# Every order table of a five-engine GNN kernel is redrawn: head, first, steady, last and end

## The chip, the cores and the metric

One core of a Trainium2 chip runs the program. The metric is the device time of one execution in microseconds. A median of three executions stands for a kernel; one more execution was taken with the profiler. TensorE appears as PE (weight loads as PEld), VectorE as DVE, ScalarE as ACT, GpSimd as POOL, and SyncE, which issues the DMAs, as SP.

## The reference, cut to what matters

Two graph layers over 128 graphs (NB) of 128 nodes (N) and 64 features (F), 192 hidden columns (H) in the first.

```python
mask = (adj > 0.0)                                  # layer 0
h = relu((x @ W1a)[:, :, None] + (x[:, :, None] - x[:, None]) @ W1b + b1)   # each pair j, k
x = layernorm(x + einsum('bjkh,bjk->bjh', h, mask) @ W2 + deg * b2)
m = relu(relu(x @ W1 + b1) @ W2 + b2)               # layer 1
msg = relu(adj @ m)
r, z = sigmoid(i_r + h_r), sigmoid(i_z + h_z)       # i from msg, h from x
x = layernorm(x + (1 - z) * tanh(i_n + r * h_n) + z * x)
```

## The kernel before

**Tiling.** Graphs are taken four at a time: q = 0..31 (NQ = 32) is a quad. Layer 0 does not visit all pairs of nodes. For each quad a table of neighbours is made, and nine rounds of matmuls gather one neighbour each into PSUM; VectorE then does accumulator = accumulator + max(PSUM, 0). A quad has two halves, A (accumulator AC, `round_a`) and B (accumulator BB, `round_b`). Of each half ScalarE does round 1 (a plain relu, L1602 and L1618), VectorE rounds 2 to 9 (L1203 and L1223). Rounds 2 to 6 are 1152 columns wide, rounds 7 and 8 768, round 9 480.

**Turns.** Turn t (0 to 32) runs half B of quad t-1 and half A of quad t side by side: b1, a1, b2, a2, ... b9, a9. While VectorE accumulates one half's round from its PSUM banks, TensorE makes the other half's next round. Around these go, for other quads and groups of eight graphs (g, u):

- `prep(t+1)` (letter p): `x_split`, `ov`, `rank_t`, `rank_ov`, `words` (VectorE, tile WM, L1172), `x_turn`, `v` and `v_low` twice, `v_out` (SP copies VN to VA and VB), `surplus`. The DMA of `words` fills CW, from which `dgen(t, m)`, m = 0..3 (digits 0 to 3; VectorE, tile DM, L1182), makes the one-hot tables of turn t. `dgen(t, 0)` is needed by b1 and a1 of turn t, `dgen(t, 1)` by b2 and a2, and so on. On POOL the step `dgen` is a wait: POOL does not go on before that DM is made.
- `seeds(t)` (letter s): the first PSUM contents of half A of quad t, made after b9 of the turn before; ScalarE takes them off (L1626) before a1 may write.
- `parts_of_u` (b), `tail` (t: `s_ov`, `out0_a`, `out0_b`, `out0_c` of quad t-2), `ranks` (r: `mask`, two `rank_n`, `split_x`, `count`, `off`), `load` (l).
- layer 1 of a group of eight graphs, some 30 steps (`layer1_steps`): squares1, power1, scale1, xg, m1, m2, msg, the gates, tanh, gd, h, yt, y, squares2, power2, scale2, store. It starts in an odd turn (n) and is carried over the next turns (d, e).

**Order.** Each engine is in order. One list of steps made by `main_order` is followed by all five, so a letter's place in a table sets where the step stands in each engine's queue. `HEAD` is all before the first round; `FIRST` is turn 0; `ORDER[0]` the even turns and `ORDER[1]` the odd ones up to turn 30; `LAST` turns 31 and 32; `END` all after. A turn's table has 19 strings: one before b1, then one after each round of b and of a in turn.

**Banks.** PSUM banks 0 to 5 hold the rounds. All other matmul steps share banks 6 and 7: a step may write when the step that had the bank before has been taken off by its reader. The class `Banks` hands them out in the list's order, so a moved step also changes who waits for whom.

Of the kernel before, what the change touches and what calls it, by code (L numbers as in the profile page):

```python
# [53 lines left out]


ORDER = (
    ("e2p3bs", "", "rpbbd", "", "t", "p", "e", "rrp", "bt", "ptt", "pee", "edbpe", "pp", "e", "pd", "b", "d", "0", "1er"),
    ("bsb2", "", "3d", "pp", "btb", "p", "dd", "p", "tlpt", "etd", "bnbdrd", "dp", "depdn", "p", "p", "dp", "dpnr", "0", "1"),
)

FIRST = ("", "srr2hbp", "prb3", "b", "p", "", "hp", "", "bpb", "pp", "r", "pb", "r", "p", "0", "p", "p", "", "h1r")

LAST = (
    ("bbt", "b2s3dtb", "tt", "nd", "nbd", "ddn", "dbd", "nd", "", "d", "n", "d", "n", "", "ne", "de", "d01", "", "d"),
    ("bbdtb", "e", "etee", "e2dtftdnddnd", "dn", "fdded3ndde", "nf", "", "", "f", "bbn", "", "n", "", "", "df", "ene", "", "ddeb"),
)

HEAD = ("t", "WwL", "AASrXK", "EGrrr", "rr", "Mpp", "tpA", "wrtp", "ppr", "p", "ppfp0", "1pt")

END = ("d", "d", "tdlttttnndlnnn", "l", "ldnl", "l", "n", "ln", "ndnln", "llnnldt", "nl", "llnd", "lnlnnln", "l")  # L70

MAIN = (
# [119 lines left out]
def build(nc, adj, adjt, xt, xn, xq, w1, w2, rows, wg, cst, out):  # L192
    ctx = ExitStack()
    with ctx:
# [233 lines left out]
        def main_order(do):  # L428
# [82 lines left out]
            def checks():  # L511
                for k in range(5):
                    do("flag", k)
                    yield
# [31 lines left out]
            def halves(stage, n):  # L546
                for i in range(n):
# [5 lines left out]
                            "f": ("fold",), "0": ("dgen", 0, 0), "1": ("dgen", 0, 1)}  # L553
            for c in "".join(HEAD):
                if c in first_steps:
# [8 lines left out]
            for t in range(NQ + 1):  # L564
# [10 lines left out]
                if t == NQ:  # L575
                    link["n"] = layer1_steps(do, bank, NG - 1)
                    link["f"] = checks()
                order = FIRST if t == 0 else ORDER[t % 2] if t < NQ - 1 else LAST[t - NQ + 1]

# [40 lines left out]

            for c in "".join(END):
                if c in link:
# [1422 lines left out]
```

## Time and profile before

| what | us |
| --- | --- |
| median of 3 executions (812.18 to 813.53) | 813.08 |
| the profiled execution | 811.95 |
| its span, first to last instruction | 807.4 |
| start of turn 0's first accumulation on VectorE | 33.1 |
| one even and one odd turn in the steady part (turns 16 and 17) | 46.27 |
| last accumulation of half B, then the rest of the program | 785.2, 22.2 |

VectorE is the busiest engine; TensorE and ScalarE are not far behind. From turn 6 to turn 29 the trace repeats to a few hundredths of a microsecond from pair to pair, but for turns 21 and 23, so one pair stands for the steady part. In a timeline a row is: start in us, us from start to end, engine, line, operation, tiles out<-in, shapes, count, and in brackets the idle time before it with what ended it.

### The profile page before, as it was taken

What the parts mean: (1) busy time and instruction counts of PE and PEld (TensorE: products, weight loads), DVE (VectorE), ACT (ScalarE), POOL (GpSimd) and SP (SyncE); (2) the same over time, 40 slices, a digit from 0 to 9 for tenths busy, and PEclk for the clock granted to TensorE, in tenths of its full rate; (3) what the DMA queues carried; (4) which work ended last, traced back from release to release, by engine and by line L of the source; (5) the groups of instructions that cost most, each with busy time, mean ns of one, the idle gap of its engine ahead of it and who ended that gap; (6) DMA issues with size and microseconds to landing.
All of it is one profiled execution on the core that took longest, in us unless ns stands there. A gap on an engine that the chain in (4) does not pass through costs nothing.

```text
span 807.4 us, 37453 instructions
## 1 busy us (share of the span) xinstructions
PE 686.1 (85%) x15984; PEld 575.6 (71%) x15984; DVE 741.4 (92%) x817; ACT 674.4 (84%) x1931; POOL 610.7 (76%) x655
## 2 busy tenths in 40 slices
PE   1678779889898989989898898889889898989775
PEld 0557667778787877778777777777777787778653
DVE  4798989999999999999999999999999999998884
ACT  3857577889989989998989989898898999898664
POOL 4354555897979788897988889798888979776872
PEclk9999999999999999999999999999999999999998
DMA  4341322323233242323233242313324231222000
GB/s 168 84 129 42 105 69 55 106 64 106 49 93 81 56 120 69 100 68 100 57 76 103 64 119 55 115 35 100 89 56 115 65 109 45 59 68 55 16 15 27
DMA packets 33317, 62.67 MB, mean 78 GB/s; under 512 B 5504, under 2 KB 14464, under 8 KB 33152
## 3 DMA queue, kind: packets, MB, share of 16 engines
q1 hardware_dynamic: 33152, 60.29, 27.3%
q8 instruction: 126, 2.06, 1.1%
q14 instruction: 39, 0.32, 0.1%
HBM read 22.52 MB, written 4.19 MB: 33 GB/s over the span
## 4 chain that ended last, share of the span: by engine, by line
PE 44%; ACT 27%; issue 14%; DVE 11%; POOL 2%; DMA 1%; POOLq 0%; SPq 0%; DVEq 0%; ACTq 0%
PE PS L653 34%; PE PS L910 5%; PE PS L975 4%; DVE BB L1223 4%; DVE AC L1203 3%; ACT AC L1602 3%; ACT BB L1618 3%; ACT VN L1571 2%; ACT NNB L1586 2%; ACT SD L1626 2%; ACT NNB L1583 2%; ACT YO L1490 2%; ACT X L1407 1%; ACT XT L1558 1%; ACT Q L1505 1%
## 5 line engine op out<-in xcount | busy, mean ns | idle before, releaser
L1223 DVE SCALAR_TENSOR_TENSOR BB<-PS,BB 128x1152 f32<-128x1152 f32 (+4 forms) x256 | 293.0, 1145 | 29.2 <-PE PS L653 27.2
L1203 DVE SCALAR_TENSOR_TENSOR AC<-PS,AC 128x1152 f32<-128x1152 f32 (+4 forms) x256 | 292.2, 1141 | 1.9 <-PE PS L910 1.9
L653 PE MATMUL PS<-DM,VA 128*64 128x192 fp8e5 (+1 forms) x2048 | 127.5, 243 | 36.1 <-ACT SD L1626 18.5
L653 PEld LDWEIGHTS PS<-DM,VA 128*64 128x64 f16 x2048 | 82.8, 109 | 70.0 <-DVE AC L1203 28.0
L653 PE MATMUL PS<-DM,VB 128*64 128x192 fp8e5 (+1 forms) x2048 | 124.9, 241 | 0.3
L1182 DVE TENSOR_SCALAR DM<-CW 128x1536 uint16<-128x1536 uint16 (+1 forms) x132 | 112.3, 881 | 1.0 <-DMA CW<-WM 1.0
L1862 POOL TENSOR_TENSOR SD<-SD,BB 128x512 f32<-128x512 f32 (+1 forms) x62 | 77.9, 1275 | 36.1 <-DVE DM L1182 36.1
L910 PE MATMUL PS<-DM,VB 128*64 128x192 fp8e5 (+1 forms) x1024 | 85.7, 242 | 22.4 <-DVE BB L1223 17.2
L653 PEld LDWEIGHTS PS<-DM,VB 128*64 128x64 f16 x2048 | 91.1, 111 | 1.0 <-DVE BB L1223 0.5
L910 PE MATMUL PS<-DM,VA 128*64 128x192 fp8e5 (+1 forms) x1024 | 84.4, 240 | 0.4 <-DVE AC L1203 0.2
L910 PEld LDWEIGHTS PS<-DM,VB 128*64 128x64 f16 x1024 | 50.0, 110 | 40.5 <-issue 21.0
L1854 POOL TENSOR_TENSOR SD<-SD,AC 128x512 f32<-128x512 f32 x64 | 64.2, 1004 | 0.0
L1832 POOL TENSOR_TENSOR XE<-XQ,XT 128x512 f16<-128x512 f32 x32 | 37.6, 1176 | 30.8 <-ACT XT L1558 15.9
L1847 POOL TENSOR_TENSOR SD<-SD,NNB 128x512 f32<-128x512 f32 x64 | 58.1, 921 | 0.0
L1800 POOL TENSOR_SCALAR MT<-AT 128x1024 bf16<-128x1024 f32 x15 | 41.8, 2785 | 19.5 <-PE PS L653 18.7
L910 PEld LDWEIGHTS PS<-DM,VA 128*64 128x64 f16 x1024 | 50.8, 110 | 1.5 <-DVE AC L1203 1.2
L653 PE MATMUL PS<-w2s,SD 128*64 128x64 f32 (+1 forms) x768 | 48.2, 250 | 0.0
L1537 ACT ACTIVATE AM<-PS 64x512 int16<-64x512 f32 x64 | 37.6, 588 | 11.6 <-PE PS L653 11.0
L975 PE MATMUL PS<-w2s,AC 128*64 128x64 f32 x512 | 36.4, 225 | 4.0 <-ACT MS L1437 3.5
L975 PEld LDWEIGHTS PS<-w2s,AC 128*64 128x64 f32 x512 | 32.3, 138 | 9.8 <-ACT MS L1437 6.3
L1571 ACT ACTIVATE VN<-PS 128x384 f16<-128x384 f32 x64 | 31.6, 493 | 7.5 <-PE PS L653 6.2
L653 PEld LDWEIGHTS PS<-w2s,SD 128*64 128x64 f32 x768 | 37.7, 138 | 0.0
(243 smaller groups left out, 2203.7 us busy)
## 6 DMA issues: line engine op xcount, KB each, us to landing
CW<-WM SPq DMA_DIRECT2D x128, 160.0 KB, 2.8
XQ<-in_xq SPq DMA_DIRECT2D x32, 256.0 KB, 2.6
AT<-in_adjt SPq DMA_DIRECT2D x15, 512.0 KB, 4.0
VA<-VN SPq DMA_DIRECT2D x64, 96.0 KB, 2.2
VB<-VN SPq DMA_DIRECT2D x64, 96.0 KB, 2.2
XN<-in_xn SPq DMA_DIRECT2D x16, 256.0 KB, 4.1
out<-YO SPq DMA_DIRECT2D x15, 256.0 KB, 3.1
WG<-in_wg SPq DMA_DIRECT2D x1, 515.5 KB, 5.9
```

The costliest lines, as they stand in the source:

```text
L653: last = e.matmul(o[k], lhs[:, k], rhs, **flags)
L910: last = e.matmul(PS[h:h + 64, b + 2, 256 * (i // 2) + cols.start:256 * (i // 2) + cols.stop], lhs[:, i, k:k + 64], d[:, i, :], start=Fals ...
L975: last = e.matmul(PS[64 * h:64 * h + 64, b, 64 * i:64 * i + 64], lhs, w2s[:, w, :], start=(w == 0), stop=(w > 0))
L1182: e.tensor_scalar(DM[m][:, halves], CW[t % 3][:, halves, first], 6 - 2 * m, 0xC0C0, ALU.logical_shift_left, ALU.bitwise_and).then_inc(s["d ...
L1203: e.scalar_tensor_tensor(t, tiles(PS[:, b + p:b + 3, :])[:, :, cols], 0.0, t, ALU.max, ALU.add).then_inc(s["sx"], 1)
L1223: e.scalar_tensor_tensor(t, tiles(PS[:, r, :])[:, :, cols], 0.0, t, ALU.max, ALU.add).then_inc(s["sy"], 1)
L1537: e.activation(graphs(am[k])[:, :, 64 - 64 * h:192 - 64 * h], src[k], ACT.Copy, scale=2.0, bias=-258.0)
L1571: e.activation(VN[q % 2][:, 0, k:4:2, 0:H], PS[:, b, :].rearrange("p (a n) -> p a n", a=2)[:, :, 0:H], ACT.Copy).then_inc(s["vh"], 1)
L1800: e.tensor_scalar(MT[g % 3][:], AT[g % NA][:], 0.0, None, ALU.is_gt).then_inc(s["mask"], 1)
L1847: e.tensor_tensor(u, u, NNB[:, 4 * k:4 + 2 * k, :], ALU.mult).then_inc(s["im"], 1)
L1854: e.tensor_tensor(u, u, AC[q % 3][:, h, nat], ALU.add).then_inc(s["aa"], 1)
L1862: e.tensor_tensor(u, u, BB[q % 2][:, h, 0:128], ALU.add).then_inc(s["ad"], 1)
```

## The change

The five order tables are replaced. No step is added, removed or altered, and no function is touched; what changes is the place of each step in the five queues and, by that, which of banks 6 and 7 it gets.

```diff
 ORDER = (
-    ("e2p3bs", "", "rpbbd", "", "t", "p", "e", "rrp", "bt", "ptt", "pee", "edbpe", "pp", "e", "pd", "b", "d", "0", "1er"),
-    ("bsb2", "", "3d", "pp", "btb", "p", "dd", "p", "tlpt", "etd", "bnbdrd", "dp", "depdn", "p", "p", "dp", "dpnr", "0", "1"),
+    ("2se", "3b", "rppe", "", "bdb", "t", "p", "p", "ebe", "per", "pt", "rteptre", "p", "dp", "b", "d", "pbe", "", "01r"),
+    ("sl", "bb", "23t", "bd", "", "bppp", "ddbe", "p", "pttb", "tpr", "dnnd", "dd", "pnd", "p", "dn", "p", "", "dp", "dp01e"),
 )
-FIRST = ("", "srr2hbp", "prb3", "b", "p", "", "hp", "", "bpb", "pp", "r", "pb", "r", "p", "0", "p", "p", "", "h1r")
+FIRST = ("sph2", "3", "pbb", "", "", "bbp", "", "pb", "", "r", "pb", "rrr", "pp", "r", "ph", "p", "p", "0p", "1hr")
 LAST = (
-    ("bbt", "b2s3dtb", "tt", "nd", "nbd", "ddn", "dbd", "nd", "", "d", "n", "d", "n", "", "ne", "de", "d01", "", "d"),
-    ("bbdtb", "e", "etee", "e2dtftdnddnd", "dn", "fdded3ndde", "nf", "", "", "f", "bbn", "", "n", "", "", "df", "ene", "", "ddeb"),
+    ("bbts", "bdtb2", "", "ttnb", "ddn3", "e", "bdddn", "dddn", "", "d", "", "dn", "d", "", "end", "", "01n", "", ""),
+    ("fbbtbfde", "efet2ebf", "3", "ettn", "dnddddd", "ned", "e", "", "", "fdn", "den", "nbd", "", "", "ndd", "n", "", "bddee", ""),
 )
-HEAD = ("t", "WwL", "AASrXK", "EGrrr", "rr", "Mpp", "tpA", "wrtp", "ppr", "p", "ppfp0", "1pt")
-END = ("d", "d", "tdlttttnndlnnn", "l", "ldnl", "l", "n", "ln", "ndnln", "llnnldt", "nl", "llnd", "lnlnnln", "l")
+HEAD = ("L", "Xrr", "SrAAEWrrK", "rrG", "tArw", "ppw", "tp", "ptpt", "p", "f", "M", "p", "ppp0p1")
+END = ("ld", "ltllllt", "ltnt", "ntndlnl", "nd", "nllnltn", "nnld", "ldlnll", "dnn", "nd", "lnn", "nn", "nd")
```

Read out for one even turn, 16, the lists give (a slot is what stands behind the round named):

- before: a1 rank_n, ov; a2 s_ov; b3 rank_t; a3 split_h; b4 rank_ov; a4 out0_a; b5 words, out0_b, out0_c; a5 x_turn, yt twice; b6 y, xg, v, squares2; a6 v_low, v; b7 squares2, power2; a7 v_low, m1; a8 m2; b9 dgen(17, 0); a9 dgen(17, 1), off, v_out, surplus, seeds(17).
- after: a1 rank_n, x_split, ov, split_h; a2 xg; b3 s_ov; a3 rank_t; b4 rank_ov; a4 yt twice; b5 words, y, rank_n; a5 x_turn, out0_a; b6 split_x, out0_b, squares2, v, out0_c, count, squares2, power2; a6 v_low; b7 m1, v; b8 m2; a8 v_low; a9 dgen(17, 0), dgen(17, 1), off, v_out, surplus, seeds(17).

At the end of an odd turn, 17: before, surplus, scale1 and rank_n stand after a8, dgen(18, 0) after b9, and after a9 dgen(18, 1), h, dgen(18, 2), x_split(19), dgen(18, 3), seeds(18); msg stands before b2 of the odd turn. After: tanh and v_low stand after b9; after a9 gd, v_out, surplus, dgen(18, 0) to (18, 2), seeds(18), h, then b1, dgen(18, 3); msg stands behind b2, and s_ov before it. In the head, the mask's loads now stand first and the weights' later, and `wide_w(0)` behind `off` on VectorE.

## Rows read from the trace of the kernel before

**Rows 1.** The page's first part: busy us (share of the span) x instructions

```profile
PE 686.1 (85%) x15984; PEld 575.6 (71%) x15984; DVE 741.4 (92%) x817; ACT 674.4 (84%) x1931; POOL 610.7 (76%) x655
```

**Rows 2.** Windows of turns 16 and 17: stretch, its us, each engine's busy us

```profile
394.99:412.87 17.88, 16.11 (x420) 13.79 (x420) 17.77 (x17) 15.96 (x53) 16.55 (x24) 1.00 0.27 69
412.87:417.98 5.11, 4.57 (x101) 4.32 (x97) 5.11 (x7) 5.07 (x12) 3.14 (x2) 1.00 0.13 31
417.98:436.22 18.24, 17.03 (x408) 14.05 (x403) 17.78 (x18) 16.24 (x52) 15.09 (x14) 1.00 0.40 115
436.22:441.26 5.04, 4.04 (x82) 3.45 (x82) 4.02 (x6) 4.96 (x10) 4.41 (x3) 1.00 0.27 64
```

**Rows 3.** VectorE's groups by form, 394.99:441.26: busy us, mean ns | idle before

```profile
L1223 DVE SCALAR_TENSOR_TENSOR BB<-PS,BB 128x1152 f32<-128x1152 f32 x11 | 14.9, 1354 | 2.5 <-PE PS L653 2.5
```

**Rows 4.** VectorE's timeline at the end of turn 17 and the start of 18

```profile
437.16 3.08 DVE L1182 TENSOR_SCALAR DM<-CW 128x1536 uint16<-128x1536 uint16 x3
441.26 1.36 DVE L1223 SCALAR_TENSOR_TENSOR BB<-PS,BB 128x1152 f32<-128x1152 f32 x1 [1.02 <-PE PS L653]
```

**Rows 5.** TensorE's timeline in the same stretch: seeds and b2

```profile
436.27 0.63 PE L653 MATMUL PS<-XE,wxh 128*64 128x256 f16 x8 [0.22 <-DVE BB L1223]
...
440.53 0.36 PE L910 MATMUL PS<-DM,VB 128*64 128x192 fp8e5 x4
```

**Rows 6.** ScalarE's timeline in the same stretch: XT, relu of b1

```profile
437.84 0.63 ACT L1558 ACTIVATE XT<-XQ 64x512 f16<-64x512 f32 x1
...
439.25 1.14 ACT L1618 ACTIVATE BB<-PS 128x1152 f32<-128x1152 f32 x1
```

**Rows 7.** POOL's timeline: second step of count beside words; gd beside DM

```profile
404.10 0.73 POOL L1698 TENSOR_TENSOR CT<-CT,Q 128x16 f32<-128x16 f32 x1
...
436.17 1.64 POOL L1760 TENSOR_TENSOR GT<-GT,GZ 128x512 f32<-128x512 f32 x1
```

**Rows 8.** VectorE's timeline in the head: wide_w(0), mask, count, words

```profile
5.50 0.42 DVE L1236 TENSOR_SCALAR wuv<-wa 128x192 f32<-128x192 f32 x1 [5.50 <-DMA wa<-in_w]
...
8.71 2.93 DVE L1150 TENSOR_SCALAR MT<-AT 128x512 bf16<-128x512 f32 x2
...
15.60 0.17 DVE L1696 TENSOR_SCALAR CT<-Q 128x16 f32<-128x16 bf16 x1 [3.96 <-ACT Q L1505]
...
23.84 0.83 DVE L1172 TENSOR_TENSOR WM<-c,AM 128x1280 uint16<-128x1280 uint16 x1
```

**Rows 9.** TensorE's timeline at the first round

```profile
31.61 0.52 PE L653 MATMUL PS<-DM,VA 128*64 128x192 fp8e5 x8 [2.37 <-DMA VA<-VN]
```

**Rows 10.** ScalarE's groups by form, 394.99:441.26

```profile
L1407 ACT ACTIVATE X<-XR,st 128x64 f32<-128x64 f32 x8 | 2.1, 339 | 0.0
...
L1648 ACT ACTIVATE SY<-GT 128x512 f16<-128x512 f32 x1 | 0.6, 642 | 0.0
...
L1416 ACT ACTIVATE XGh<-PS 128x512 f16<-128x512 f32 x1 | 0.6, 597 | 0.3 <-PE PS L653 0.3
```

**Rows 11.** TensorE's timeline in turn 16: out0_b, a5, v, a6

```profile
402.09 0.57 PE L653 MATMUL PS<-b2x,MT 128*64 128x64 bf16 x24
...
403.18 0.53 PE L653 MATMUL PS<-DM,VA 128*64 128x192 fp8e5 x8
...
405.49 0.35 PE L653 MATMUL PS<-br,on 128*64 128x384 bf16 x2
...
406.07 0.52 PE L653 MATMUL PS<-DM,VA 128*64 128x192 fp8e5 x8
```

**Rows 12.** SyncE's timeline in turn 16: the two copies of VN to VA

```profile
410.20 1.10 SPq L1924 DMA_DIRECT2D VA<-VN  x2
```

**Rows 13.** The page's DMA issues: KB each, median us from issue to landing

```profile
VA<-VN SPq DMA_DIRECT2D x64, 96.0 KB, 2.2
```

**Rows 14.** VectorE's timeline in turn 32: b2, then scale1(15, 0) before b3

```profile
767.34 1.02 DVE L1218 SCALAR_TENSOR_TENSOR BB<-PS,BB 128x384 f32<-128x384 f32 x2 [3.56 <-PE PS L910]
...
772.65 0.43 DVE L1090 TENSOR_TENSOR X<-XR,st 128x256 f32<-128x256 f32 x1 [1.92 <-POOL st L1729]
```

## The prediction

> **What bounds the kernel now.** I read the page's first part, then windows of one pair of turns, then who ended VectorE's waits, then the timelines of the four engines at the two turn ends. VectorE is busy 92% of the span, ScalarE 84%, TensorE 85% [rows 1]. The windows cut a pair of 46.27 us into two long stretches, from the start of round 2 to the end of b9 (17.88 even, 18.24 odd), and two turn ends (5.11 and 5.04) [rows 2]. They have different limits.
>
> In the long stretches VectorE runs almost without a break; half B's 11 full rounds waited 2.5 us in the window, 1.02 of that at its right edge, in the odd-to-even turn end, and again at its left edge, from the end before [rows 3, 4]. So inside a pair only about 0.5 us of stretch idle is to be had.
>
> A turn end is a chain, not VectorE's load: b9 taken off, seeds on TensorE (436.27), b1, ScalarE's relu of b1 (439.25 to 440.39), b2 (440.53), and the next accumulation at 441.26 [rows 4, 5, 6]. VectorE makes its DM tables meanwhile: three take 3.08 us, POOL's gd and h alternating with them (gd's product takes 1.64 us of it) [rows 4, 7]; then it still waits 1.02 us for TensorE. A faster DM there is worth nothing. What lengthens the chain is ScalarE: XT (0.63 us from 437.84) stands before the relu of seeds, so the relu of seeds can't start before 438.5 and that of b1 follows at 439.25, though TensorE, 1.5 us in seeds and 1.0 in b1, had both by 438.8 [rows 5, 6].
>
> **The change part by part.**
>
> *Head.* Before, VectorE runs the weights' step first (5.50 to 8.71), then the two masks, 2.93 us since the POOL memsets of setup run beside them; the counting starts at 15.60, and words at 23.84 [rows 8]. TensorE's first round waits 2.37 us for the copied VA and starts at 31.61 [rows 9]. After, the mask's load is issued first, so it lands about 0.9 us sooner, near 5.2 us, and no weights' work stands before it: masks end near 6.8 instead of 11.6, `rank_n` stands no more behind `rank_t`, and counting starts near 8.4, 7.2 earlier. The 3.2 us of `wide_w(0)` (8.71 - 5.50) now come behind `off`, beside the chain of ov and rank_ov, whose ScalarE queue has got `rank_t` in front instead; that gives about 1 us back. I follow words to 17.4 (6.4 earlier), v to about 17.5, VA's copy and the first round to 25.2. Every term after that is as before, so the head gives -6.4; I take **-6.0**, since POOL's mask(1), count and the second load are now late and stand in turn 0. Bounds: -7.2 (all that counting gains) to -3.2 (only `wide_w` moved).
>
> *Even turns, long stretch.* Three queues shift. First, ScalarE between its relu of a1 and the end of `rank_t`'s AM: it loses scale1 (4 x 0.24 us start to start) and one 512-column copy, and gains XT, SY and the pair XGh and XG [rows 6, 10]: -1.6 + 2.15 = +0.5 us, and SY waits some 0.3 us for POOL's h, which now starts later. AM ends some 0.9 us later after round 2's start. Now yt, before b5, uses the bank of `rank_t` and waits for just that; of the 0.9, slack takes all but 0.2 us, by which VectorE's fifth round is late. Second, slot b6 holds out0_b, out0_c and v: 403.18 - 402.09 = 1.09 and 406.07 - 405.49 = 0.58, so 1.67 us, with out0_a and x_turn (about 1.0) before b6 [rows 11]. A full round of VectorE is 1.265 start to start and TensorE's round 0.50, so a slot has 0.765 us free and 0.5 can be saved up: a6 is about 0.35 us late. Third, v(1) stands in b7, on the bank of v(0), whose low half ScalarE takes off only after both squares2 (0.96 us each): a7 about 0.3 late, a8 0.1. A fourth, 0.1, is b4. Sum 1.05; the old stretch has 0.35 of such gaps. The stretch also hands dgen(17, 0) (0.47) to the turn end. But the length asked is to b9's end, where that DM never was: **+0.7 us** (17.9 to 18.6).
>
> *Even-to-odd turn end.* dgen(17, 0) now sits on the chain, as b1 waits for it; but seeds (1.33 us of TensorE) run beside it and end later than it. VectorE has one DM more, 0.47, and AC9 before it is no longer preceded by that DM. From b9's end both come out at 5.1: **0**, bounds -0.2 and +0.5.
>
> *Odd stretch.* out0_a with out0_b in one slot as before; squares1 twice ahead of the sigmoid of gate_i. I find 0.7 us of gaps against 0.5, and one DM less: **0**, bounds -0.4 and +0.8.
>
> *Odd-to-even turn end.* XT and `rank_n`'s Q leave the place before seeds on ScalarE; surplus (1.25 us) and v_low come into it instead. seeds end 1.5 us after b9, b1 a microsecond later, relu 1.14, b2 0.7: 4.7 against 5.04, **-0.33**. DM(18, 0), which b1 needs, meets POOL's gd and waits for it; it is done just as seeds are. Two covers are thin here. VA's second copy is issued some 0.5 us after v_low and lands 2.2 later [rows 12, 13], and v_low(1) now is one of the last steps on ScalarE, so a1 gets VA 0.2 us after it wants it, by my reckoning. And ScalarE has no idle time from squares1 on. Uncovered they cost 0.5 us each.
>
> So a pair goes from 46.27 to 46.65, **+0.4**; 13 pairs with layer 1 in them (turns 4 to 29) give **+5.5**.
>
> *Last turns and end.* In turn 31 out0_b and out0_c move behind b2: its start is 1.1 us sooner, but three gates in slot a3 then cost about 1. In turn 32, VectorE idles 3.56 us before b2 and 1.92 before b3 for POOL's power [rows 14]; after, the flag steps and both DMs fill the first and scale1 goes behind b3, so VectorE is through 2 us sooner. But s_ov stands behind yt(14), which waits for POOL's h(14), not moved: only 0.3 of it arrives. power1(16) goes ahead of power2(14) on POOL: -0.6. **-1.0**, bounds -3 and +1.
>
> Sum against the profiled execution: 811.95 - 6.0 + 5.5 - 1.0 = 810.45, and 1.13 more for the median: **811.6**.
>
> **One rule beside the trace.** POOL's second count step took 0.73 us beside words, where it is one of the 0.2 us kind, so it waited for VectorE's WM; the reverse, WM waiting for a POOL add, does not occur in the steady part, since WM always found POOL idle or in short steps [rows 7]. The Trainium skill, page "SBUF — State Buffer", section "Who interferes with whom", says that a VectorE instruction with two SBUF inputs and a GpSimd one that reads SBUF exclude each other for the whole instruction, in both directions. By that rule the new table pays at words, and it is the third rival.
>
> **The rivals.**
>
> 1. *ScalarE becomes the bound* (slower). The two thin covers fail, and the even turn's gaps are 0.2 us longer: the pair is +0.95 and the time 813.1 - 7 + 13 x 0.95 = **818.5**. It decides from a pair of 46.8 on. For it: ScalarE is busy 5.07 of 5.11 and 4.96 of 5.04 us in the turn ends. Against: in the long stretches it has 17.88 - 15.96 + 18.24 - 16.24 = 3.9 us of slack a pair [rows 2].
> 2. *The stretch gaps don't come* (faster). They are sums of 0.1 to 0.4 us steps, each on a bank that may be free just in time. Then +0.1 and -0.33 leave -0.25 a pair: 813.1 - 7 - 3 = **803**.
> 3. *words meets POOL's adds.* In the even turn POOL's add_a, SHL and add_a now run where WM wants to start; what is left of one when WM comes is 0.2 to 1.0 us (gd's product took 1.64 and the short step 0.73 with the other in the way [rows 7]), and I take 0.45. It covers part of the sixth round's gap. 13 x 0.45 = 5.9 more: **817.5**.
> 4. *The head gives nothing*: v or VA's copy is held by something I moved wrongly (br, XE, the banks): **817**.
>
> **How the numbers follow.** Forecast 0.42, with a range of its own of 807.6 to 815.6; rival 1 0.20, rival 2 0.24, rival 3 0.10, rival 4 0.04. About 0.2% is what a measurement of this kernel can tell from no change, that is 1.6 us. The forecast lies at -0.18%, so it is split: 0.21 faster, 0.15 same, 0.06 slower. Faster 0.21 + 0.24 = 0.45; same 0.15; slower 0.06 + 0.34 = 0.40. The range 803 to 820 leaves out the far halves of rivals 1 to 3, under 0.2.
>
> **What would show it.** In the profile after: the first round on TensorE near 25 us instead of 31.6 (head); a pair of 46.4 to 46.9 (steady); in the even turn, waits of VectorE for TensorE before rounds 5, 6 and 7, with TensorE held by a ScalarE release; the odd-to-even end at 4.7. WM longer than 0.9 us is rival 3; a pair over 46.8 with a1 waiting for VA or seeds' relu late is rival 1; a pair under 46.2 is rival 2. The prediction is wrong in kind if the head's gain is not there, or if a turn end is not a chain through ScalarE's relu.

## The result and the profile after

The median is 813.77 us against 811.82 for the kernel before on the same chip, 20 executions each: a ratio of 1.0026, 95% interval 1.0017 to 1.0035. It is 0.26% slower, where I had forecast 0.18% faster; 813.77 lies in my range. The profiled execution took 813.3 us with a span of 808.8, against 811.95 and 807.4. One of the six executions of e16 below took 861.72 us at a mean granted clock of 0.789 and is left out of its ratio. Where the 1.4 us of span came from (us; turn t starts here with ScalarE's relu of its a1, L1602, the step that fills accumulator AC, and "first accumulation" means that step of turn 0 from here on):

| stretch | before | after | difference | predicted |
| --- | --- | --- | --- | --- |
| start to first accumulation | 32.8 | 25.9 | -6.9 | -6.0 |
| turns 0 to 3 | 82.6 | 82.4 | -0.2 | 0 |
| turns 4 to 30 | 628.2 | 637.3 | +9.1 | +5.5 |
| turn 31 to the end | 63.8 | 63.2 | -0.6 | -1.0 |

The split between the last two rows hangs on the mark. Counted from VectorE's own first accumulation of each turn the four differences are -6.6 (33.11 to 26.55), -0.6, +8.1 and +0.5: at turn 31 VectorE starts 0.4 us after that relu in the changed kernel and 1.5 us after it before.

Busy time of the page, and the windows of turns 16 and 17 (stretch, its us, then busy us of PE, PEld, DVE, ACT, POOL), which answer to [rows 1, 2]:

```profile
PE 692.2 (86%) x15984; PEld 569.7 (70%) x15984; DVE 749.6 (93%) x817; ACT 670.9 (83%) x1931; POOL 599.7 (74%) x655
```

```profile
392.99:411.49 18.50, 16.47 (x428) 14.00 (x428) 18.27 (x17) 16.32 (x53) 16.64 (x24) 1.00 0.22 53
411.49:416.63 5.14, 5.04 (x124) 4.81 (x120) 5.14 (x6) 4.93 (x12) 3.15 (x2) 1.00 0.34 80
416.63:434.85 18.22, 16.23 (x374) 13.03 (x370) 17.95 (x17) 16.35 (x56) 14.70 (x13) 1.00 0.35 97
434.85:439.93 5.08, 4.39 (x90) 3.40 (x84) 4.33 (x7) 4.35 (x8) 3.89 (x4) 1.00 0.47 129
```

A pair of turns takes 46.94 us, 0.67 more than before. VectorE executes the same 817 instructions and yet is busy 1.01 us longer in the pair (45.69 against 44.68), while its idle time fell from 1.59 to 1.25. In the even stretch alone VectorE's idle time went from 0.11 to only 0.23 us. So the first thing to look for is not a new wait but an instruction that got longer. In the even turn it is WM (VectorE's rows of the even and the odd turn, then the one wait of VectorE inside the even stretch, then POOL's rows beside WM):

```profile
401.89 1.36 DVE L1172 TENSOR_TENSOR WM<-c,AM 128x1280 uint16<-128x1280 uint16 x1
...
424.45 0.83 DVE L1172 TENSOR_TENSOR WM<-c,AM 128x1280 uint16<-128x1280 uint16 x1
```

```profile
409.96 0.96 DVE L1203 SCALAR_TENSOR_TENSOR AC<-PS,AC 128x768 f32<-128x768 f32 x1 [0.23 <-PE PS L910]
```

```profile
401.19 0.69 POOL L1841 TENSOR_TENSOR SHL<-SO,SHL 128x256 f16<-128x256 f32 x1
401.82 0.75 POOL L1854 TENSOR_TENSOR SD<-SD,AC 128x256 f32<-128x256 f32 x1
```

POOL's add_a began 0.07 us before WM and ended at 402.57; WM then took 1.36 us instead of the 0.83 of the odd turn (0.82 on the mean in the kernel before). This repeats: WM takes 1.26 to 1.38 us in 12 of the 13 even turns from 6 to 30 and 0.82 in the other, turn 12, where add_a has only 0.11 us left when WM starts. At the odd-to-even turn end it is DM(18, 0) and DM(18, 1), which answer to [rows 4, 7] (the first row is DM(18, 0) in the kernel before):

```profile
436.13 0.55 DVE L1182 TENSOR_SCALAR DM<-CW 128x1536 uint16<-128x1536 uint16 x1
```

```profile
435.43 1.27 DVE L1182 TENSOR_SCALAR DM<-CW 128x1536 uint16<-128x1536 uint16 x1
...
436.63 1.62 DVE L1182 TENSOR_SCALAR DM<-CW 128x1536 uint16<-128x1536 uint16 x1
...
439.93 1.36 DVE L1223 SCALAR_TENSOR_TENSOR BB<-PS,BB 128x1152 f32<-128x1152 f32 x1 [0.74 <-PE PS L653]
```

```profile
435.02 1.27 POOL L1757 TENSOR_TENSOR GT<-XG,GN 128x512 f32<-128x512 f32 x1
436.37 1.47 POOL L1760 TENSOR_TENSOR GT<-GT,GZ 128x512 f32<-128x512 f32 x1
```

All four DMs take hardly longer than before (3.75 us in one run of them, against 0.55 and 3.08), but before, the first took 0.55, the second 1.06 and the last 1.62 us, and now the two long ones stand first. TensorE had finished seeds at 436.40, but b1, whose program waits for DM(18, 0), starts at 436.81, 0.11 us after that DM's end at 436.70 (the profile names no releaser for this wait, so that the DM holds b1 is read from the program and tested in e5). ScalarE, early as forecast (seeds' relu starts 1.51 us after the end of b9's accumulation, against 2.27), stands idle before the relu of b1:

```profile
436.02 0.38 PE L893 MATMUL PS<-XE,wxl 128*64 128x256 f16 x4
436.81 0.41 PE L653 MATMUL PS<-CW,VA 128*64 128x128 fp8e5 x8 [0.40 <-issue]
```

```profile
436.36 0.87 ACT L1626 ACTIVATE SD<-PS 128x512 f32<-128x512 f32 x2
437.93 1.13 ACT L1618 ACTIVATE BB<-PS 128x1152 f32<-128x1152 f32 x1 [0.69 <-PE PS L653]
```

The rest of the 9.1 us is a handful of turns out of the pattern, as there are before (before 5, 21 and 23, 2.7 us in all; after 5, 11, 12, 14, 21 and 29, 3.0 us). At the ends of turns 11 and 12 it is a1 waiting for VA's copy, 0.90 and 1.12 us; in turn 21 of the kernel before TensorE stopped for 1.15 us within one step, for nothing that the trace shows (e1, e3, e4 and e11 below, with the old ORDER, stop at the same step for 1.21 to 1.51 us).

### The profile page after: what moved, and what is told of

It is laid out like the page before. It is cut to its first block, busy times and chain, and to the rows that moved or that the text cites. A ratio compares the mean times of both kernels' runs of the same rounds, so it can differ in the third digit from the quotient of the medians.

```text
span 808.8 us, 37467 instructions
## 1 busy us (share of the span) xinstructions
PE 692.2 (86%) x15984; PEld 569.7 (70%) x15984; DVE 749.6 (93%) x817; ACT 670.9 (83%) x1931; POOL 599.7 (74%) x655
## 4 chain that ended last, share of the span: by engine, by line
PE 29%; issue 20%; DVE 19%; ACT 15%; POOL 11%; DMA 3%; SPq 1%; POOLq 0%; DVEq 0%; ACTq 0%
PE PS L653 21%; DVE AC L1203 7%; DVE BB L1223 5%; POOL MT L1800 4%; PE PS L910 4%; DVE DM L1182 4%; ACT X L1407 4%; POOL st L1729 3%; DMA VA<-VN 3%; PE PS L975 2%; ACT AC L1602 2%; DVE SI L1162 2%; ACT BB L1618 1%; ACT VN L1576 1%; ACT SQ L1654 1%
## 5 line engine op out<-in xcount | busy, mean ns | idle before, releaser
L910 PEld LDWEIGHTS PS<-DM,VB 128*64 128x64 f16 x1024 | 48.2, 109 | 63.8 <-DVE BB L1223 28.4
L653 PEld LDWEIGHTS PS<-DM,VB 128*64 128x64 f16 x2048 | 91.1, 110 | 2.3 <-DVE BB L1223 1.3
L1800 POOL TENSOR_SCALAR MT<-AT 128x1024 bf16<-128x1024 f32 x15 | 41.8, 2785 | 24.2 <-PE PS L653 23.0
L1618 ACT ACTIVATE BB<-PS 128x1152 f32<-128x1152 f32 (+1 forms) x32 | 35.6, 1113 | 11.8 <-PE PS L653 9.5
L1602 ACT ACTIVATE AC<-PS 128x1152 f32<-128x1152 f32 (+1 forms) x32 | 35.4, 1108 | 3.0 <-PE PS L910 2.9
```

The costliest lines, as they stand in the source:

```text
L653: last = e.matmul(o[k], lhs[:, k], rhs, **flags)
L910: last = e.matmul(PS[h:h + 64, b + 2, 256 * (i // 2) + cols.start:256 * (i // 2) + cols.stop], lhs[:, i, k:k + 64], d[:, i, :], start=Fals ...
L1602: e.activation(ac_[:, 2 * p:6, front], tiles(PS[:, b + p:b + 3, :])[:, :, front], ACT.Relu).then_inc(s["sx"], 1)
L1618: e.activation(t, tiles(PS[:, r, :])[:, :, back], ACT.Relu).then_inc(s["sy"], 1)
L1800: e.tensor_scalar(MT[g % 3][:], AT[g % NA][:], 0.0, None, ALU.is_gt).then_inc(s["mask"], 1)
```

## The experiments

Starting theory: each table's effect can be measured alone and the effects add, the loss is all in ORDER, and inside ORDER it is VectorE meeting POOL at WM and at DM(18, 0). All runs with their ratio to the kernel before; then, from the one profiled execution of each, the span, the start of the first accumulation, and the medians over turns 6 to 29 of the even stretch, the even-to-odd end, the odd stretch and the odd-to-even end (us), these four by VectorE's timeline, cut as in [rows 2]:

| kernel | ratio (95%) | span | first | even | end | odd | end |
| --- | --- | --- | --- | --- | --- | --- | --- |
| before | 1 | 807.4 | 32.8 | 17.88 | 5.11 | 18.24 | 5.04 |
| changed | 1.0026 (1.0017-1.0035) | 808.8 | 25.9 | 18.49 | 5.14 | 18.22 | 5.07 |
| e1 new HEAD | 1.0025 (1.0017-1.0034) | 809.7 | 34.4 | 17.88 | 5.11 | 18.24 | 5.04 |
| e2 new ORDER | 1.0075 (1.0057-1.0093) | 814.8 | 32.2 | 18.49 | 5.15 | 18.21 | 5.06 |
| e3 new LAST, END | 1.0007 (0.9997-1.0017) | 808.2 | 32.2 | as before | | | |
| e4 new HEAD, FIRST | 0.9937 (0.9924-0.9950) | 802.9 | 25.7 | 17.88 | 5.11 | 18.24 | 5.04 |
| e5 dgen early | 0.9963 (0.9947-0.9979) | 803.9 | 25.4 | 18.38 | 5.15 | 18.22 | 4.72 |
| e6 add_a late | 0.9971 (0.9958-0.9985) | 804.4 | 25.6 | 18.17 | 5.14 | 18.28 | 5.06 |
| e7 XT behind a1 | 1.0033 (1.0018-1.0049) | 810.0 | 32.2 | 18.52 | 5.11 | 18.24 | 4.49 |
| e8 e4 + e7 | 0.9938 (0.9916-0.9959) | 803.3 | 25.5 | 18.52 | 5.11 | 18.24 | 4.49 |
| e9 e5 + e6 | 0.9943 (0.9922-0.9964) | 804.3 | 26.0 | 18.38 | 5.14 | 18.26 | 4.73 |
| e10 e9, v first | 1.0075 (1.0054-1.0095) | 816.4 | 26.2 | 18.96 | 5.21 | 18.50 | 4.72 |
| e11 e1, rank_n late | 0.9941 (0.9921-0.9961) | 803.9 | 25.5 | 17.89 | 5.11 | 18.26 | 5.04 |
| e12 e8, scale1 late | 1.0300 (1.0274-1.0326) | 834.2 | 26.0 | 20.80 | 5.11 | 18.24 | 4.49 |
| e13 e4, Q early | 0.9896 (0.9877-0.9915) | 797.9 | 25.8 | 17.87 | 5.23 | 18.49 | 4.49 |
| e14 e4, add_b, msg late | 1.0052 (1.0035-1.0069) | 810.3 | 25.6 | 17.89 | 4.68 | 19.50 | 5.04 |
| e15 e13 + e14 | 1.0016 (1.0002-1.0030) | 807.0 | 25.7 | 17.89 | 4.68 | 19.80 | 4.49 |
| e16 e5, add_b late | 0.9933 (0.9915-0.9952) | 801.7 | 25.8 | 18.38 | 4.64 | 18.52 | 4.72 |
| e17 e9, yt late | 0.9953 (0.9938-0.9969) | 805.8 | 26.1 | 18.40 | 5.14 | 18.23 | 4.72 |
| e18 e16, add_a, yt late | 0.9944 (0.9922-0.9965) | 802.8 | 25.9 | 18.40 | 4.85 | 18.50 | 4.73 |

### One table at a time (e1 to e4, e11)

e1 takes only HEAD of the change, e2 only ORDER, e3 only LAST and END, e4 HEAD and FIRST, all on the kernel before; their diffs are the parts of the change's.

> The kernel before with the new HEAD alone; FIRST, ORDER, LAST and END as before. Theory (the head's gain is real, and the steady tables gave it away): in the changed kernel turn 0's first accumulation came 6.9 us sooner (25.9 against 32.8 us), but turn 0 was 1.1 us longer (16.1 against 15.0). With the old FIRST behind it the head's late steps (the second load, mask(1), count) must be caught up in turn 0 as well, so I expect 5.5 to 7 us off the kernel before: about 805.5. Rival (the head only shifts a wait that turn 0 or 1 has anyway): under 3 us off, turns 0 and 1 together 4 us longer or more. Second rival (the trace of the changed kernel misleads, its loss sits in the head): no gain or a loss.

> The kernel before with the new ORDER (turns 1 to 30) alone. Theory: the whole loss is here. A pair of turns goes from 46.27 to 46.93 us, 13 or 14 times, so 8 to 9.5 us are added: about 821. Rival (the pair's loss comes from the new head or FIRST, which leave the carried steps or the banks in another phase): the pair stays at 46.3 to 46.5 and the kernel is within 3 us of the kernel before.

> The kernel before with the new LAST and END alone. Theory: in the changed kernel the stretch from turn 31 to the end was 63.2 us against 63.8, so 0 to 1 us off, about 811.3; my prediction said 1.0 off. Rival: the new LAST fits the new ORDER's phase only (which layer-1 steps are still open at turn 31), and behind the old ORDER it is slower by 1 us or more.

> The kernel before with the new HEAD and the new FIRST; ORDER, LAST and END as before. It tells what FIRST is worth. Theory (FIRST only catches up what the new head left late, and does it better than the old FIRST): 0.5 to 1.5 us faster than the kernel with the new HEAD alone, near 804.5, with turn 0 at about 16 us. Rival (FIRST is neutral, turn 0's extra 1.1 us is the head's late work however it is placed): equal to it within 0.5 us.

e2 confirms that the pair's loss is ORDER's own, whatever stands before it: its four medians are those of the changed kernel to 0.01 us. Its time, 819.0 us, is 2 us less than I expected. e3 can't be told from no change; from turn 31 its profile took 65.0 us against 63.8, which suggests that the new LAST fits the new ORDER better, by one profile. e1 refuted me: the new HEAD with the old FIRST has its first accumulation at 34.4 us, later than before. TensorE's timeline tells why (e1, seeds, then rank_n):

```profile
22.52 0.40 PE L893 MATMUL PS<-XE,wxl 128*64 128x256 f16 x4
31.64 0.64 PE L653 MATMUL PS<-cs,MT 128*64 128x128 bf16 x8 [8.71 <-POOL MT L1800]
```

The old FIRST has rank_n(2) ahead of a1. It reads mask(1), whose input the new HEAD loads late, and TensorE, in order, stands there for 8.71 us with the first round behind it. The new FIRST has rank_n(2) and (3) behind b6. e11 is e1 with mask(1) and these two rank_n moved behind b5 and a5 (both lines are cut short):

```diff
-FIRST = ("", "srr2hbp", "prb3", "b", "p", "", "hp", "", "bpb", "pp", "r", ...
+FIRST = ("", "s2hbp", "pb3", "b", "p", "", "hp", "", "bpb", "ppr", "rrr", ...
```

> The kernel before with the new HEAD alone, as the first run of the study, and in FIRST the mask of group 1, rank_n(2) and rank_n(3) moved from around round a1 of turn 0 to behind b5 and a5. Theory (the head's gain was lost with the old FIRST because TensorE, in order, stood 8.7 us at rank_n(2) for POOL's mask(1), whose input loads late in the new HEAD): the first accumulation is back at 25.5 to 26.5 us instead of 34.4, and the kernel is at 806 to 809 us. Rival (it is something else of FIRST, such as v_out or the bias steps): first accumulation still later than 30 us, time unchanged at 814.

The first accumulation is at 25.5, and the kernel, 0.9941, is as fast as e4. So the head's gain was real, and the place of rank_n decided whether it arrived. e4 also refutes what I had expected of FIRST: it is worth 6.5 us on top of the new HEAD, not 0.5 to 1.5.

The parts don't add up: spans of e4, e2 and e3 are -4.5, +7.4 and +0.8 us against before, +3.7 together, where the whole change is +1.4. Turns 1 and 2 are part of it: 22.32 and 22.16 us before, 23.30 and 23.29 in e4, 21.71 and 22.17 in the changed kernel; why is not settled.

### VectorE meets POOL (e5, e6, e9)

On the changed kernel; e5 the first edit, e6 the second, e9 both. Slots are counted from 0.

```diff
-ORDER[1][17:19] = "dp", "dp01e"
+ORDER[1][17:19] = "0dp", "dp1e"
...
-ORDER[0][8], ORDER[0][12] = "ebe", "p"
+ORDER[0][8], ORDER[0][12] = "ee", "pb"
```

> The changed kernel with dgen(t+1, 0) of the odd turns moved from behind the last round of half A to ahead of it, behind b9 (as in the kernel before). Theory (the odd-to-even turn end did not shorten, 5.07 instead of my 4.7 us, because DM(18, 0) ran at the same time as POOL's gd and took 1.27 us instead of 0.55, so that b1 waited for it): the DM now starts at about 434.9, before or just as POOL begins gd, b1 starts some 0.4 us sooner and the end is 4.5 to 4.7 us; 13 pairs x 0.4 to 0.5 = 5 to 6.5 us off the changed kernel, about 1.002 less the 0.0070: some 808 us. Rival (the end is ScalarE's or TensorE's chain: seeds, relu, b1, whatever the DM does): the end stays at 5.0 or more, b1 then waits for ScalarE's relu of seeds, and the time is unchanged at 813.8. Second rival (VectorE's total of DM time sets it: the meeting with POOL only moves to another DM): DM(18, 0) short but DM(18, 1) or a9 long, end 4.9 to 5.1.

> The changed kernel with add_a(t-1, 1), a POOL addition of 256 columns, moved in the even turns from ahead of words to behind count. Theory (words' WM took 1.36 us instead of 0.82 because it met that addition, and this is what makes the even stretch 18.49 us): WM back to 0.82 to 0.85, even stretch 17.95 to 18.1, 13 x 0.45 = 6 us off the changed kernel, about 808. Rival (WM's length only fills the gap in which VectorE would have waited for TensorE's sixth round; my prediction put about 0.9 us of such waits in this stretch): WM at 0.82, but waits of VectorE for TensorE before rounds 6 to 8 of 0.4 us or more in its place, stretch unchanged at 18.4 to 18.5, time unchanged.

> The changed kernel with both moves, dgen(t+1, 0) ahead of the odd turn's last round of half A and add_a(t-1, 1) behind count in the even turns. Each alone brought the span from 808.8 to 803.9 and 804.4 us. Theory (two meetings of VectorE with POOL in two places, each with its own price: 0.35 us at the odd-to-even end, 0.32 in the even stretch): they add, a pair of 46.26 us, 13 pairs x 0.67 = 8.7 off, span near 800, about 805.5 us. Rival (one slack feeds both, so that the second brings only what the first left): a pair of 46.5 or more, about 808.

e5 brought the end to 4.72 and 4.9 us of span. VectorE's rows of turn 17's end, and TensorE's first round of half A:

```profile
432.57 0.70 DVE L1182 TENSOR_SCALAR DM<-CW 128x1536 uint16<-128x1536 uint16 x1
...
437.38 1.36 DVE L1223 SCALAR_TENSOR_TENSOR BB<-PS,BB 128x1152 f32<-128x1152 f32 x1 [0.33 <-PE PS L653]
```

```profile
434.04 0.39 PE L653 MATMUL PS<-CW,VA 128*64 128x128 fp8e5 x8
...
435.72 0.52 PE L653 MATMUL PS<-DM,VA 128*64 128x192 fp8e5 x8 [0.68 <-DMA VA<-VN]
```

DM(18, 0) is made ahead of a9's accumulation, b1 follows seeds at once (434.04), and the next thing in the chain is what I had named a thin cover: a1 waits 0.68 us for VA, and b2 stands behind a1. In the changed kernel DM(18, 0) hid most of that wait; 0.30 us of it is left there, before a1's weight load. POOL now meets DM(18, 1) instead (1.28 us), as my second rival said, but nothing in the chain waits for that one.

e6 put WM back to 0.82 us, but only 0.32 of the 0.54 us came; the rest VectorE waited for TensorE, about 0.20 us before its sixth round of half A and 0.25 before the seventh. So theory and rival are both right in part:

```profile
399.85 0.82 DVE L1172 TENSOR_TENSOR WM<-c,AM 128x1280 uint16<-128x1280 uint16 x1
...
405.80 0.96 DVE L1203 SCALAR_TENSOR_TENSOR AC<-PS,AC 128x768 f32<-128x768 f32 x1 [0.25 <-PE PS L910]
```

e9, both moves, gave nothing over e5 that can be told (spans 804.3 and 803.9; ratios 0.9943 and 0.9963, whose intervals overlap), and its pair of 46.51 us is the rival's. Why e6's edit had nothing left to shorten stands in e5's own trace, in the even turn (VectorE, POOL):

```profile
400.00 0.89 DVE L1172 TENSOR_TENSOR WM<-c,AM 128x1280 uint16<-128x1280 uint16 x1
```

```profile
399.53 0.68 POOL L1841 TENSOR_TENSOR SHL<-SO,SHL 128x256 f16<-128x256 f32 x1
400.16 1.32 POOL L1854 TENSOR_TENSOR SD<-SD,AC 128x256 f32<-128x256 f32 x1
```

In e5 the earlier end shifted the two queues against each other: WM starts 0.16 us ahead of add_a instead of 0.07 behind, and now POOL waits (1.32 instead of 0.75 us) and WM doesn't. But e5's even stretch is 18.38 us, not the 18.17 of e6: with WM as short, the rounds wait for TensorE instead (0.25 us before the seventh of half A in e5 too). So of WM's 0.54 us the stretch gained 0.32 in e6 and 0.11 in e5.

### What else holds the even stretch (e10, e17, e18)

With WM short, the changed order's even stretch stays at 18.38 to 18.40, half a microsecond over 17.88. I tried two places where TensorE waited there: e10 is e9 with the first edit, e17 is e9 with the second, e18 is e16 (below) with that of e6 and the second.

```diff
-ORDER[0][11:13] = "rteptre", "pb"
+ORDER[0][11:13] = "rtptr", "peeb"
...
-ORDER[0][8:10] = "ee", "per"
+ORDER[0][8:10] = "", "peeer"
```

> The kernel of the run beside it (both moves), and in the even turns squares2 twice and power2 behind v(17, 0) and v_low(17, 0), not among them. Theory (my term for banks and v in the even stretch is right: with WM back at 0.82 us only 0.32 of 0.54 us came, because VectorE then waited 0.20 us before its sixth round of half A and 0.25 before the seventh for TensorE, which is held by v on the bank that ScalarE takes off only behind the squares): the wait before the seventh round goes, even stretch 17.9 to 18.0 us, 2 to 3 us off. Rival (those waits are TensorE's own load in slot b6, out0_b, out0_c and v together, and not the bank): no change within 0.05 us a turn.

> The kernel with both moves (dgen ahead of a9, add_a behind count; 807.7 us, span 804.3, even stretch 18.38), and in the even turns yt twice moved from ahead of b5 to behind words, ahead of y. Theory (TensorE, in order, stands 0.61 us at yt for ScalarE's AM, with b5 and all rounds behind it waiting; this was the first of my four terms): b5 no longer waits, even stretch 18.0 to 18.15, 3 to 4.5 us off, about 804. Rival (slot a5 gets too full: yt, y and rank_n ahead of a5, then out0_a, x_turn ahead of b6, so that the wait moves to rounds 5 and 6; the sum of TensorE's work and not the place sets the stretch): stretch 18.3 or more, no gain.

> All four moves on the changed kernel: dgen ahead of a9 and add_b behind dgen(t, 3) in the odd turns (those two alone 807.1 us, span 801.7), add_a behind count and yt behind words in the even ones. Theory (different places, different causes, the gains add but for what the second end gives back to the odd stretch): a pair of about 45.9 us, span near 797, 802 us. Rival (what is given in one place is waited for in the next, as with dgen and add_a together, which gave nothing over dgen alone): 806 or more.

In e10 the wait before the seventh round went, as my term for v and the banks says, but nothing was gained: a worse one came before the eighth (VectorE, TensorE), and the stretch is 18.96 us where I had expected 17.9 to 18.0:

```profile
410.98 0.96 DVE L1203 SCALAR_TENSOR_TENSOR AC<-PS,AC 128x768 f32<-128x768 f32 x1 [0.91 <-PE PS L910]
```

```profile
409.32 0.41 PE L653 MATMUL PS<-br,on 128*64 128x512 bf16 x2 [0.40 <-ACT M L1424]
```

Both squares2 now stand on ScalarE ahead of m1's relu (M, L1424), and m2, ahead of a8, waits for it. In e17 TensorE's 0.61 us wait at yt for AM is gone and nothing is gained; the seventh round of half A waits just as in e6 (VectorE, then TensorE):

```profile
406.57 0.96 DVE L1203 SCALAR_TENSOR_TENSOR AC<-PS,AC 128x768 f32<-128x768 f32 x1 [0.25 <-PE PS L910]
```

```profile
398.11 0.36 PE L910 MATMUL PS<-DM,VB 128*64 128x192 fp8e5 x4 [0.58 <-DVE BB L1223]
400.60 0.22 PE L653 MATMUL PS<-cs,XE 128*64 128x64 f16 x2 [0.18 <-ACT Q L1505]
```

After yt moved TensorE waits 0.58 us at b5 for VectorE instead, so the 0.61 us had been slack: in this order of steps it was not on the path. e18 gave nothing over e16 either (0.9944 and 0.9933), where I had expected another 5 us. What sets the last half microsecond of that stretch is not settled; what is left in its rows are small waits for ScalarE's queue (Q, 0.18 us, and VN).

### The turn ends (e7, e8, e12, e13 to e16)

e7 is the kernel before with the first edit, e8 has the new HEAD and FIRST besides, e12 is e8 with the second.

```diff
-ORDER[0][0], ORDER[0][2] = "e2p3bs", "rpbbd"
+ORDER[0][0], ORDER[0][2] = "e23bs", "rppbbd"
...
-ORDER[0][2], ORDER[0][8], ORDER[0][11], ORDER[0][13] = "rppbbd", "bt", "edbpe", "e"
+ORDER[0][2], ORDER[0][8], ORDER[0][11], ORDER[0][13] = "rppbb", "dbt", "ebpe", "de"
```

> The kernel before with x_split of the even turns moved from ahead of seeds' relu to behind round a1: one letter. Theory (the odd-to-even turn end is a chain through ScalarE's relus, in which XT stands for 0.63 us): the end goes from 5.04 to 4.4 to 4.6 us and 13 pairs bring 6 to 8 us, 804 to 806 us, if POOL and ScalarE have room for the step behind a1. Rival (the wait is passed on: VectorE's DMs, 3.08 us, and POOL's gd and h set the end as well, or XT behind a1 delays ov and rank_t and so the rounds behind it): the end is shorter by under 0.3 us or the even stretch is longer by what the end gains; 810 to 812 us.

> The kernel before with the new HEAD and FIRST, which together were 0.63% faster (807.7 us), and with x_split moved as in the run beside it. Theory (the two are far apart in time and simply add): 4.5 + 6 to 8 us off the kernel before, about 800 us. Rival (the part gained in the steady turns is lost where the carried steps are in another phase: with the new HEAD and FIRST turns 1 and 2 were 1 us longer each): less than 8 us off in all, 804 or more.

> The kernel before with new HEAD and FIRST and x_split behind a1 (807.2 us), and in the even turns scale1(u, 1) and split_x1 moved from behind a1 to behind a4, xg from b6 to b7. Theory (moving x_split took 0.55 us off the odd-to-even end but put 0.63 us on ScalarE ahead of rank_t's AM, which is what made the even stretch 18.52 instead of 17.88 us): with 1.7 us of ScalarE work taken out of that place the even stretch is at 17.9 to 18.1 us, the end stays at 4.49, 13 x 0.5 = 6.5 us off, about 801. Rival (the even stretch is lengthened by POOL, where XE now comes behind the addition of BB, or by xg and what hangs on it coming too late): stretch still 18.4 or more, time at 807 or later.

e7 took the end from 5.04 to 4.49, as a chain through ScalarE's relus would have it, and the even stretch grew by 0.64. XT now stands before AM on ScalarE, and TensorE waits for AM at out0_a, ahead of b5 (VectorE's row is BB's of that round):

```profile
400.76 0.22 PE L653 MATMUL PS<-cs,XE 128*64 128x64 f16 x2 [0.62 <-ACT AM L1541]
```

```profile
402.17 1.36 DVE L1223 SCALAR_TENSOR_TENSOR BB<-PS,BB 128x1152 f32<-128x1152 f32 x1 [0.29 <-PE PS L653]
```

e8 adds to e4 as little (0.9938 and 0.9937). e12 meant to relieve ScalarE there and made it 2.3 us worse, against my expectation: xg moved to b7, and m1 behind it waits 2.09 us until v_low has freed the bank that m1 takes (TensorE):

```profile
416.45 0.41 PE L653 MATMUL PS<-XGh,HH 128*64 128x512 f16 x2 [2.09 <-ACT VN L1576]
```

The second path to a shorter end is to take Q out of it, into a place where ScalarE idles (e13, the first edit, on e4); or, at the other end, to take POOL's additions out of VectorE's way (e14, the second, on e4; e15 both on e4; e16, the third, on e5):

```diff
-ORDER[1][11], ORDER[1][16] = "dp", "dpnr"
+ORDER[1][11], ORDER[1][16] = "dpr", "dpn"
...
-ORDER[1][0], ORDER[1][2:4] = "bsb2", "3d", "pp"
+ORDER[1][0], ORDER[1][2:4] = "s2", "3bb", "dpp"
...
-ORDER[1][1:3] = "bb", "23t"
+ORDER[1][1:3] = "", "23bbt"
```

> The kernel before with the new HEAD and FIRST (807.7 us, span 802.9), and rank_n of the odd turns moved from behind a8 to behind b6, where ScalarE waited 0.55 us for TensorE. Its Q (0.69 us) stood in the odd-to-even end ahead of seeds' relu. Theory (the end is ScalarE's chain; and the even stretch was lengthened in the kernel with x_split behind a1 because ScalarE got the work there instead, which is not so here): end 4.4 to 4.6 instead of 5.04, even stretch 17.9, odd stretch 18.24 to 18.4, 5 to 7 us off, 801 to 803. Rival (the even stretch is tied to something that does not move with the end, such as POOL's gd, h and the addition of BB, so that an earlier start is waited off): even stretch 18.3 or more, no gain.

> The kernel before with the new HEAD and FIRST, and in the odd turns both add_b (POOL) moved from around seeds to behind dgen(t, 3), and msg (TensorE, 1.07 us) from ahead of b2 to behind it. Theory (the even-to-odd end, 5.11 us, is VectorE's SI and DMs, of which two take 2.64 us because they take turns with POOL's additions, and behind it TensorE's msg ahead of b2): the DMs take 0.5 us each, the end is 4.3 to 4.6 us, 6 to 9 us off, 799 to 802. Rival (ScalarE's relus set the end: relu of b1 ended at 416.6, so that b2 can't start before; and POOL, which now makes its additions in the odd stretch, hands the delay to the mask, the count and the gates): end 4.9 or more, or odd stretch longer by what the end gains.

> Both edits of the two runs beside it together. Theory (two turn ends, two causes, independent): the gains add, 11 to 16 us off the kernel with new HEAD and FIRST, 792 to 797. Rival (one slack: ScalarE has only some 4 us a pair, and what one end gives the other takes): no more than the better of the two alone plus 1 us.

> The changed kernel with dgen(t+1, 0) ahead of the odd turn's last round of half A (809.8 us, span 803.9), and in the odd turns both add_b moved from behind b1 to behind dgen(t, 3). Theory (as for the run with the same move in the old order: the 5.14 us of the even-to-odd end are VectorE's, 1.1 us of it waits for POOL's additions): end 4.5 to 4.7, 6 us off, about 803.5. Rival (TensorE's s_ov ahead of b2 or ScalarE's relu of b1, 413.97 to 415.1, is next in line at once): end 5.0 or more, time unchanged at 809.

e13 is the best of the study, 803.55 us, 0.9896 of the kernel before (0.9877 to 0.9915). The end is 4.49 and the even stretch unchanged at 17.87; the odd stretch gave back 0.25 and the other end 0.12. ScalarE's rows: Q in its gap and the wait that is left behind it, then seeds' relu, which now starts 1.71 us after the end of b9's accumulation (before, 2.27):

```profile
421.60 0.69 ACT L1505 ACTIVATE Q<-PS,cs 128x512 bf16<-128x512 f32 x1
422.74 0.60 ACT L1458 ACTIVATE M<-PS 128x512 f32<-128x512 f32 x1 [0.46 <-PE PS L653]
...
429.53 0.87 ACT L1626 ACTIVATE SD<-PS 128x512 f32<-128x512 f32 x2
```

Of its 5.0 us of span against e4, 2.7 came by the start of turn 4 (107.1 against 109.8), in turns 1 and 2 mostly, and 2.6 in turns 4 to 30.

e14 shows that POOL stretches the even-to-odd end: with add_b behind the DMs, two DMs take 1.02 us and POOL's two additions 1.96. In the changed kernel they take turns, and as good as the same in the one before, 2.64 and 3.14 us (VectorE, POOL, of the changed kernel):

```profile
414.06 2.65 DVE L1182 TENSOR_SCALAR DM<-CW 128x1536 uint16<-128x1536 uint16 x2
```

```profile
413.15 3.15 POOL L1862 TENSOR_TENSOR SD<-SD,BB 128x512 f32<-128x512 f32 x2 [2.14 <-DVE DM L1182]
```

In e14 the end fell to 4.68, where it waits for TensorE, whose b2 waits for ScalarE's relu of b1. But msg behind b2 took 1.07 us in front of a2, and the odd stretch paid 1.26 us (VectorE, e14):

```profile
412.21 1.02 DVE L1182 TENSOR_SCALAR DM<-CW 128x1536 uint16<-128x1536 uint16 x2
414.34 1.36 DVE L1223 SCALAR_TENSOR_TENSOR BB<-PS,BB 128x1152 f32<-128x1152 f32 x1 [1.11 <-PE PS L653]
415.92 1.36 DVE L1203 SCALAR_TENSOR_TENSOR AC<-PS,AC 128x1152 f32<-128x1152 f32 x1 [0.23 <-PE PS L910]
418.12 1.36 DVE L1223 SCALAR_TENSOR_TENSOR BB<-PS,BB 128x1152 f32<-128x1152 f32 x1 [0.84 <-PE PS L653]
```

e15 has both ends short, 4.68 and 4.49, and pays in the odd stretch (19.80): no faster than the kernel before, where I had expected 11 to 16 us off e4. e16, without msg in the way, has the end at 4.64 and gives back 0.30 in the odd stretch: 2.2 us of span less than e5, where I had expected about 6.

## Why the prediction was wrong, and where it was right

I forecast 0.18% faster and it came 0.26% slower: one step, the shorter odd-to-even turn end, did not happen, because b1 had to wait for a DM that POOL held up, and my sum of the pair left that wait out.

*Head, -6.0: right in mechanism, -6.9 measured.* Masks, counting, and a first round 7 us sooner came as followed. The first round on TensorE starts at 24.58 us, where I had 25.2. What the step left out is its condition. I wrote that mask(1) and the second load "are now late and stand in turn 0" and put that at nothing; e1 shows its price when the cover is not there, 8.71 us, the whole gain. FIRST was no part of my sum at all, and it carries it.

*Even stretch, 17.9 to 18.6: 18.49, the right number by luck.* I had four small waits for TensorE, 1.05 us less the 0.35 of such gaps in the old stretch. VectorE's idle time there went only from 0.11 to 0.23 us, the longest wait being 0.23, and 0.54 us is WM's. That is rival 3, with 0.54 where I had 0.45, and as I had said it "covers part of the sixth round's gap": with it gone (e6) 0.32 came back and 0.29 over before stayed, and in e5 and e9, where the turn end comes sooner, 0.5 stayed, as waits for TensorE. So the gaps that I had summed are there in part, but behind WM, and not beside it. Of the four terms the first was shown not to be on the path (e17); the third names a wait that is there and that went when the steps moved, but the move cost more than it gave (e10).

*Even-to-odd end, 0: right, 5.11 to 5.14.* e14 and e16 show what I had not seen, that VectorE's two DMs are stretched there by POOL, 1.6 us for two, in both kernels.

*Odd stretch, 0: right, 18.24 to 18.22.*

*Odd-to-even end, -0.33: the failed step.* Measured 5.04 to 5.07. I had written that DM(18, 0) "meets POOL's gd and waits for it; it is done just as seeds are", and so put b1's wait for it at nothing. It was 1.27 us long, not 0.55, and done at 436.70, 0.3 us after seeds; b1 started 0.4 us late, and ScalarE idled 0.69 us. The other terms were right: seeds ended 1.55 us after b9 (I had 1.5), b1 took 1.0, the relu 1.13, b2 to the next accumulation 0.7. They add up to 4.3, not to the 4.7 that I wrote; the hand-overs between them, which I did not name, measured 0.25, and b1's wait is the remaining 0.4. With the DM ahead of gd (e5) the end is 4.72, the 4.7 that I had forecast, though a1's wait for VA is in it. e5, where the step holds, is at 809.8 us and on the side that I had forecast. It is no pure test: its even stretch is 0.11 us shorter too, since WM no longer meets add_a.

*The sum.* 0.7 - 0.33 is 0.37 a pair, and 13 pairs of it are 4.8 us, not the 5.5 that I wrote. By the windows of turns 16 and 17 the pair is off by 0.37 at this end, by -0.08 in the even stretch, by 0.03 at the other end and by -0.02 in the odd stretch, 0.30 in all; 13 x 0.30 = 3.9 us. That and 0.4 us from the turns out of the pattern are what turns 4 to 30 are off by (9.1 against 4.8). The head's extra 0.9 us hid part of it.

*The last turns, -1.0: -0.6 by one mark, +0.5 by the other.* Before b2 of turn 32 VectorE no longer waits (3.56 us in [rows 14]), its flag steps and DMs fill it, but 1.55 us of waiting came before b3. By VectorE's marks turn 30, which ends with b2 of turn 31, is 0.85 us shorter, turn 31 0.97 longer, and the rest 0.5 shorter: -0.4 together, with the first two near what I had worked out (1.1 and about 1).

*The rivals.* Rival 1, the thin cover of VA: at the ends of turns 11 and 12 of the changed kernel a1 waited 0.90 and 1.12 us for it, at the end of turn 17 only its weight load, 0.30 us, behind the DM; at the same end in e5 it waited 0.68. Rival 2 did not come. Rival 3 did, at 0.10 the least likely but one, and it is what made the even stretch come out as forecast. The Trainium skill, page "SBUF — State Buffer", section "Who interferes with whom", says that issue order and not the kind of operation decides who blocks; the traces agree for these two: add_a 0.07 us ahead and WM pays 0.54, WM 0.16 us ahead (e5) and add_a pays 0.57. I had weighed the rule and given it a tenth, since WM met nothing before. The right question was whether it would still meet nothing.

## What to carry to other kernels

When a table of steps is redrawn, compare busy time per instruction before idle time: the same 817 instructions were 8.2 us longer busy, which no list of waits shows. Where VectorE and GpSimd met here, which of them started first was decided by tenths of a microsecond, so price such a meeting on both outcomes, and look whether an edit elsewhere shifts it. Work taken out of a chain gains only where it lands in idle time: e13 took Q from a full ScalarE stretch to a place where ScalarE waited, and gained; e7 and e14 moved theirs to where other steps were waited for, and paid it all back. And price a sum of small waits as a guess: the four of the even stretch came out right only because another cost stood in their place.

## What the runs showed of the hardware that I had not expected

The price of a meeting can be read off beforehand. In every meeting of WM or a DM with POOL that I worked out, VectorE's instruction is longer by what is left of POOL's TENSOR_TENSOR when it starts, less 0.14 us. In the changed kernel add_a has 0.68 us left and WM pays 0.54, in turn 30 0.58 and 0.44, in turn 12 0.11 and nothing; DM(18, 0) finds 0.86 left and pays 0.72, DM(18, 1) 1.21 and 1.07. In e5 WM finds 0.21 us of SHL and pays 0.07.

Where both engines have work queued they take turns, and both pay. At the even-to-odd end of the changed kernel VectorE's SI and two DMs alternate with POOL's two additions: the two DMs took 2.65 us, and 1.02 when POOL was not there (e14), the additions 3.15 and 1.96, so 1.6 and 1.2 us more.

Not every POOL operation does it: in e1 the WM at 58.01 us took 0.81 us while POOL's mask (L1800, a TENSOR_SCALAR of 1024 columns) was under way from 56.95 to 59.72. The kernel before shows the same in turn 1 (WM 0.82 us at 56.34, the mask from 55.34 to 58.11). Why this one leaves WM alone is not settled.
